# A ViT tower with a routed expert layer: a row table in blocks of 112, a reordered last tile, earlier first weights

## What is computed

```python
h = tok(x)                                   # layernorm, projection, layernorm, class row, positions
h = h + attn(layernorm(h))                   # q k^T / 256, diagonal masked, softmax, v
xf = layernorm(h)
topv, topi = top_k(softmax(xf @ router_w + router_b), 2); topv /= topv.sum()
pv, pp = top_k(where(flat_i == expert, flat_v, -1), 444)      # for each of the 8 experts
tok = pp // 2
out_e = (gelu(xf[tok] @ w1 + b1) @ w2 + b2) * pv              # 256 -> 1024 -> 256
out = layernorm(zeros.at[tok].add(out_e)) * ln_g + ln_b
h = h + out
```

## Time and profile before

| | before |
|---|---|
| median of 3 runs | 412.13 us (410.66 to 412.42) |
| the profiled execution | 415.01 us, of which the span from first to last instruction is 413.1 us |
| busy | PE 348.5 us (84%), DVE 315.5 (76%), ACT 255.3 (62%), POOL 224.1 (54%) |
| mean granted TensorE clock | 0.913 |
| DMA | 57.29 MB, mean 139 GB/s |
| chain that ended last, by engine | PE 60%, DVE 14%, issue 10%, POOL 8%, ACT 4% |
| its largest lines | L994 18%, L977 17%, L837 6%, L1290 2%, L805 2%, L812 2%, L939 2% |

### The profile page before, as it was taken

The page is one execution under the profiler, slowest core; times in us unless marked ns, Lnnn a source line. Parts: engine busy times, 40 slices in busy tenths (PEclk is TensorE's granted clock), DMA queues, the critical chain, the costliest instruction groups (busy, mean ns, idle before and its releaser), DMA issues.

```text
span 413.1 us, 7904 instructions
## 1 busy us (share of the span) xinstructions
PE 348.5 (84%) x2128; PEld 307.3 (74%) x2128; DVE 315.5 (76%) x874; ACT 255.3 (62%) x552; POOL 224.1 (54%) x377
## 2 busy tenths in 40 slices
PE   2799999999999998731019899999999999999960
PEld 0499988878878886431009899999999999999950
DVE  6763788787878877679879755778888888787954
ACT  3263778767777785454710478677777776868620
POOL 3243676756667665340005443158686877755675
PEclk9896999999999999865555999999999999999995
DMA  6650114454444479768702496546758585852231
GB/s 185 173 115 12 35 55 110 136 154 129 138 141 129 122 123 108 186 198 268 20 0 68 119 274 190 161 151 179 216 173 236 166 235 169 250 169 64 60 84 45
DMA packets 49278, 57.29 MB, mean 139 GB/s; under 512 B 12248, under 2 KB 38229, under 8 KB 49244
## 3 DMA queue, kind: packets, MB, share of 16 engines
q1 hardware_dynamic: 42602, 43.11, 39.4%
q0 software_dynamic: 5568, 13.00, 11.8%
q10 hardware_dynamic: 1074, 0.79, 0.8%
HBM read 36.74 MB, written 21.36 MB: 141 GB/s over the span
## 4 chain that ended last, share of the span: by engine, by line
PE 60%; DVE 14%; issue 10%; POOL 8%; ACT 4%; DMA 1%; ACTq 1%; DVEq 1%; POOLq 0%
PE pall L994 18%; PE pz L977 17%; PE pall L837 6%; DVE wproj L1290 2%; PE pall L805 2%; POOL held L1630 2%; PE pall L812 2%; PE pall L939 2%; PE pall L1005 1%; ACT stage L576 1%; PE pz L785 1%; POOL nrm L1609 1%; PE pall L963 1%; DMA bproj<-in_b_proj 1%; PE pall L777 1%
## 5 line engine op out<-in xcount | busy, mean ns | idle before, releaser
L994 PE MATMUL pall<-halves 128*128 128x444 f32 x384 | 88.6, 365 | 1.9 <-DVE halves L1398 1.9
L977 PE MATMUL pz<-halves 128*128 128x444 f32 x384 | 87.1, 362 | 0.1
L994 PEld LDWEIGHTS pall<-halves 128*128 128x128 f32 x384 | 70.8, 188 | 7.0 <-issue 1.5
L977 PEld LDWEIGHTS pz<-halves 128*128 128x128 f32 x384 | 71.9, 188 | 5.1 <-DVE halves L1409 0.2
L1649 POOL DMA_INDIRECT held<-x_rows,gidx x32 | 36.9, 1152 | 58.8 <-DVE gidx L1339 38.2
L738 ACT ACTIVATE wproj<-pz,b1t 128x444 f32<-128x444 f32 x64 | 40.5, 633 | 44.0 <-PE pz L977 43.4
L1398 DVE TENSOR_TENSOR halves<-wproj,halves 128x444 fp32r<-128x444 f32 x64 | 39.7, 621 | 27.1 <-ACT halves L750 18.7
L837 PE MATMUL pall<-halves 128*112 128x256 f32 x396 | 56.1, 298 | 3.1 <-DVE halves L1089 3.1
L837 PEld LDWEIGHTS pall<-halves 128*112 128x112 f32 x396 | 51.2, 186 | 7.2 <-DVE halves L1089 3.5
L1673 POOL DMA_INDIRECT out<-rows,didx x28 | 37.0, 1323 | 22.1 <-DVE rows L1446 15.5
L750 ACT CAST halves<-wproj 128x444 fp32r<-128x444 f32 x64 | 36.1, 564 | 2.0
(11 more groups left out here) (283 smaller groups left out, 744.5 us busy)
## 6 DMA issues: line engine op xcount, KB each, us to landing
stage<-in_w SPq DMA_DIRECT2D x32, 512.0 KB
stage<-in_x SPq DMA_DIRECT2D x64, 108.0 KB
x_rows<-x SPq DMA_DIRECT2D x22, 224.0 KB, 2.9
x_rows<-held SPq DMA_DIRECT2D x22, 224.0 KB, 4.1
sums<-rows SPq DMA_DIRECT2D x7, 448.0 KB
out<-held SPq DMA_DIRECT2D x21, 111.0 KB
x_rows<-zero SPq DMA_DIRECT2D x1, 1474.9 KB
wproj<-in_w_proj ACTq DMA_DIRECT2D x1, 768.0 KB
```

The costliest lines, as they stand in the source:

```text
L977: m = nc.tensor.matmul(bank(k % 2)[:, 0:CAP], w[:, c, k * 128:(k + 1) * 128], xs[:, e % 2, c, 0:CAP], start=(n == 0), stop=(n == 3 * EC - 1))
L994: m = nc.tensor.matmul(pall[:, 2 * (e % 2) + o, 0:CAP], w[:, k, o * 128:(o + 1) * 128], hs[:, k % 2, 0:CAP], start=(k == 0 and n == 0), st ...
```

## The change

1. **Row table.** The table has blocks of 112 rows (`P`) in place of 128, so no row of it is unused. The store of zeros at L499 goes, and `s_fill` is awaited at 32. The code of a row changes with it (`codef`, `code0`), and `read_lists` works out the block by a multiplication and a rounding in place of a mask and a shift: three more DVE instructions, each waiting for the one in front.
2. **First weights.** SP issues the four transfers of expert 0's weights at the top of step 22, ahead of that step's stores. ACT's four high halves move from the search's rounds behind its two tables.
3. **Gates.** The first gate stores move to step 24, ahead of its stores, the others to step 26; each keeps its wait on `r_V`.
4. **ACT's order.** At step 21 the scaled z of tile 21 comes ahead of x1 of tile 20. At step 22 the exponentials of tile 20 and the copy of x1T of tile 21 come directly behind x1 of tile 21, ahead of logits, x2 row and `h_rw`.
5. **POOL's order.** At step 22 POOL makes the factors of h of tile 21 alone, without waiting for tile 18's statistics, and `h_nb` before `h_dev`; tile 18's factors follow. The bias adds (L1624): tile 19's moves from step 25 to step 23 (beside tile 18's); those of tiles 20 and 21 come at step 26 behind a new wait on `r_V` = 2. Before, tiles 19 and 20 were at step 25 and tile 21 at step 26, with no such wait.

```diff
-        x2_rows = nc.dram_tensor("x2_rows", [(Q + 2) * 128, XW], fp32, kind="Internal").ap()
+        x2_rows = nc.dram_tensor("x2_rows", [(Q + 2) * P, XW], fp32, kind="Internal").ap()
@@ SP
             def step(i, slot):
                 par = slot % 2
+                if isinstance(i, int) and i == TILES:
+                    sp.wait_ge(x_n, TILES)
+                    sp.wait_ge(xT_ps, TILES)
+                    sp.wait_ge(z_ps, TILES)
+                    for h in range(2):
+                        load_w1(0, h)
+                        load_w2(0, h)
+                if isinstance(i, int) and i == TILES + 2:
+                    sp.wait_ge(r_V, 1)
+                    store_gates(0, EARLY)
+                if isinstance(i, int) and i == TILES + 4:
+                    sp.wait_ge(r_V, 2)
+                    store_gates(EARLY, TILES)
...
-                    sp.dma_start(x2_blocks[P:128, :, :],
-                                 rep(zero[0:128 - P, 0:XW].rearrange("p (a f) -> p a f", a=1), 1, Q + 2)).then_inc(s_fill, 16)
...
-            for h in range(2):
-                load_w1(0, h)
-                load_w2(0, h)
-            for a, b, n in ((0, EARLY, 1), (EARLY, TILES, 2)):
-                sp.wait_ge(r_V, n)
-                store_gates(a, b)
@@ ACT
+                last = isinstance(i, int) and i == TILES
+                if live(i - 1) and not (isinstance(i, int) and i == TILES - 1):
+                    residual_row(i - 1)
+                if last:
+                    exponentials(i - 2)
+                    turned(i - 1)
                 t = i
                 if live(t):
                     plain(act, (z_2, t + 1), (n_rs, i + 1))
                     nc.scalar.activation(tile_of(H, t), z2[:, :], ACT.Copy, scale=norm(par, 1, 0)).then_inc(z_sc, 1)
+                if isinstance(i, int) and i == TILES - 1:
+                    residual_row(i - 1)
...
             for r in range(NR - 1):
                 signs_of(r)
-                if r >= 3:
-                    (w2_high if r % 2 == 0 else w1_high)(0, (r - 3) // 2)
...
+            for pr in range(2):
+                w1_high(0, pr)
+                w2_high(0, pr)
@@ DVE, read_lists
-                V_.tensor_scalar(drow[:, 0, :], gidx[:, :], 127, None, ALU.bitwise_and)
-                link(V_.tensor_scalar(drow[:, 1, :], gidx[:, :], 8, None, ALU.logical_shift_right))
+                block_f = drow[:, 1, :].bitcast(fp32)
+                link(V_.tensor_scalar(block_f, gidx[:, :], -(P - 1) / 2.0, 1.0 / P, ALU.add, ALU.mult))
+                link(V_.tensor_scalar(block_f, block_f, BIG, None, ALU.add))
+                link(V_.tensor_scalar(drow[:, 0, :], block_f, -BIG, None, ALU.add))
+                V_.tensor_scalar(drow[:, 1, :], drow[:, 0, :], 1, None, ALU.logical_shift_right)
+                link(V_.scalar_tensor_tensor(drow[:, 0, :], drow[:, 0, :], -float(P), gidx[:, :], ALU.mult, ALU.add))
@@ POOL
+                if isinstance(i, int) and i == TILES:
+                    on = [2]
+                    pool.wait_ge(x1_ok, i - 2)
+                    pool.wait_ge(h_rw, i - 2)
+                    pool.wait_ge(h_mv, i)
+                    link(G.tensor_scalar(nrm[:, par, 0, 1:2], nmv[:, 1:2, 1], EPS, None, ALU.add))
+                    link(G.tensor_tensor(nrm[:, par, 1, 1:2], nrm[:, par, 0, 1:2], neghalf[:, :], ALU.pow))
+                    G.tensor_scalar(norm(par, 2, 1), nmv[:, 1, 0:1], norm(par, 1, 1), -1.0, ALU.mult, ALU.mult).then_inc(h_nb, 1)
+                    G.tensor_tensor(dev[:, par:par + 1], norm(par, 0, 1), norm(par, 1, 1), ALU.mult).then_inc(h_dev, 1)
...
-                for t in range(i - 6, i - 4) if isinstance(i, int) and i == TILES + 3 else (i - 5,):
-                    if live(t) and not (isinstance(i, int) and i == TILES + 2):
+                if isinstance(i, int) and i == TILES + 4:
+                    pool.wait_ge(r_V, 2)
+                for t in {TILES + 1: (i - 5, i - 4), TILES + 2: (), TILES + 3: (), TILES + 4: (i - 6, i - 5)}.get(i, (i - 5,)) \
+                        if isinstance(i, int) else (i - 5,):
+                    if live(t):
```

More of the change, by code:

```diff
@@ L475, in _, with load_w1, load_w2 @@
                 load_x(t, t)
+            HALF_H, HALF_K = HID // 2, HC // 2
+            def load_w1(e, h):
+                cols = slice(h * HALF_H, (h + 1) * HALF_H)
+                sp.dma_start(w1r[:, :, cols], w1[e].rearrange("(c p) h -> p c h", p=128)[:, :, cols])\
+                    .then_inc(w1_in[h], 16)
+            def load_w2(e, h):
+                ks = slice(h * HALF_K, (h + 1) * HALF_K)
+                sp.dma_start(w2r[:, ks, :], w2[e].rearrange("(k p) o -> p k o", p=128)[:, ks, :])\
+                    .then_inc(w2_in[h], 16)
             def step(i, slot):
                 par = slot % 2
+                if isinstance(i, int) and i == TILES:
[11 more added lines that the diff above has]
+                    store_gates(EARLY, TILES)
                 t = i + 4
@@ L555, in _ @@
             sp.wait_ge(s_out, 16 * (E - 1))
-            sp.wait_ge(s_fill, 48)
+            sp.wait_ge(s_fill, 32)
             sp.wait_ge(g_col, 64)
@@ L637, in step, with turned, exponentials @@
                                          scale=norm(par, 1, 1)).then_inc(x1_ok, 1)
+                def turned(t):
+                    need(act, x1T_ps, t + 1)
+                    need(act, s_ps, t - 1)
+                    nc.scalar.copy(x1T[:, odd, :], bank(6)[:, 0:EC * P]).then_inc(x1T_sb, 1)
+                def exponentials(t):
+                    need(act, s_nmx, t + 1)
+                    need(act, pT_ps, t)
+                    need(act, g_h, t - 1)
+                    nc.scalar.activation(prob[:, :], masked[:, :], ACT.Exp, bias=nmax[:, 0:1], scale=1.0 / ED,
+                                         accum_out=psumr[:, par:par + 1]).then_inc(p_ok, 1)
+                last = isinstance(i, int) and i == TILES
[4 more added lines that the diff above has]
+                    turned(i - 1)
                 t = i
@@ L660, in step @@
                     norm_row(t, slot, par)
-                t = i - 2
-                if live(t):
-                    need(act, s_nmx, t + 1)
-                    need(act, pT_ps, t)
-                    need(act, g_h, t - 1)
-                    nc.scalar.activation(prob[:, :], masked[:, :], ACT.Exp, bias=nmax[:, 0:1], scale=1.0 / ED,
-                                         accum_out=psumr[:, par:par + 1]).then_inc(p_ok, 1)
+                if live(i - 2) and not last:
+                    exponentials(i - 2)
                 t = i - 2
@@ L672, in step @@
                         .then_inc(h_rw, 1)
-                t = i - 1
-                if live(t):
-                    need(act, x1T_ps, t + 1)
-                    need(act, s_ps, t - 1)
-                    nc.scalar.copy(x1T[:, odd, :], bank(6)[:, 0:EC * P]).then_inc(x1T_sb, 1)
+                if live(i - 1) and not last:
+                    turned(i - 1)
             pipeline(act, step, 6, 18)
@@ L1273, in _ @@
                              ALU.mult, ALU.add)
-            V_.scalar_tensor_tensor(code0[:, :].bitcast(u16), oh12[:, 1, 0, :], 128.0, codef[:, 0:TILES], ALU.mult, ALU.add)
+            V_.scalar_tensor_tensor(code0[:, :].bitcast(u16), oh12[:, 1, 0, :], float(P), codef[:, 0:TILES], ALU.mult, ALU.add)
             dve.wait_ge(r_ka, 1)
@@ L1640, in _ @@
                 pool.wait_ge(x2_out[k], 16 * ((TILES - k + 3) // 4))
-            pool.wait_ge(s_fill, 48)
+            pool.wait_ge(s_fill, 32)
             pool.wait_ge(g_col, 64)
```

19 lines of the change are left out of this document (3 added, 16 removed).

## The result

The changed kernel took 410.63 us (median of 22 runs) where the kernel before, on the same chip, took 412.63 (22 runs): a ratio of 0.9933, interval 0.9909 to 0.9957. One of the 22 was disturbed (705.23 us) and counts for nothing. The difference of the medians is 2.0 us, the ratio gives 2.8. The forecast of 410.1 and its range hold. The profiled execution took 411.50 us, its span 409.7, against 415.01 and 413.1.

What follows compares the result with a forecast made beforehand. Bound before 235 us by a chain of waits, PE with the last tile's products, then DVE's routing. Terms 1.4 + 1.1 - 0 - 0.7 = 1.8, or 2.3; 2.0 taken from 412.13 gives 410.1 us, range 409.4 to 410.8 (8 in 10: 408.4 to 412.2).

Steps and rivals of the forecast that it cites:

- rival 1: Last tile's products: TensorE holds the high clock through L829, so 3.0 to 3.5 us faster, 409.0 us; chance 0.17.
- better case: Whole sum: 2.3 us faster if the clock falls at the same time and the adds miss the gates.
- x1 and L805: Last tile, step 22: x1, exponentials and x1T copy come earlier, so PE's L805 starts 1.4 us earlier.
- Products behind it: Last tile's products after L805: 1.4 to 2.3 us won, about 2.0 taken at the end of L829.
- Gates: DVE's gates of 16 tiles now meet two POOL adds: 0.6 us given back, bounds 0 and 1.2.
- Adds out of the routing: L1132, L1135 and L1136 in the last tiles' routing no longer run beside POOL's adds: 1.1 us won.
- Adds behind `r_V` = 2: Adds beside `keysa`: nothing to 0.7 us lost, 0 taken, since POOL needs 0.2 us to wake and `keysa` starts first.
- rival 3: At `keysa`: POOL's add gets in first and `keysa` waits for all of it, 0.7 us less gain, 410.8; chance 0.07.
- `read_lists`: Three more linked DVE instructions ahead of the first `project`: 0.66 us lost, bounds 0.5 and 0.9.
- rival 4: Gap before L994 grows to 1.8 us, TensorE's clock falls, first expert's products cost 3.7 us more, 413.8; chance 0.05.
- The fill, the weights, the gates: nothing: SP's zero fill, first weights and gate stores: no gain, as POOL's 38 us idle before the first gather covers them.

Runs made afterwards that it cites:

- G: Changed kernel with SP's old order: first weights and all gate stores behind the pipeline, no fill, blocks of 112; 409.93 us, 0.9918 to the kernel before.
- H: Changed kernel with ACT's and POOL's old order at steps 21 and 22, POOL's adds as changed; 412.67 us, 0.9993 to the kernel before.
- D: Kernel before with three redundant linked shifts added in `read_lists`, to lengthen the gap before the first `project`; 413.77 us, 1.0011 to the kernel before.
- I: Changed kernel with POOL's bias adds back at their old steps, no wait on `r_V`; 410.96 us, 0.9959 to the kernel before.
- J: Changed kernel with all four bias adds, tiles 18 to 21, behind `r_V` = 2; 410.57 us, 0.9934 to the kernel before.
- C: Changed kernel with nine idle matmuls on PE between `hidden(0, 1)` and the first `project`; 410.30 us, 0.9923 to the kernel before.
- A: The changed kernel again, unedited, for a second profile; 409.33 us, 0.9918 to the kernel before.
- K: Changed kernel with 29 idle matmuls in place of 24 ahead of the first gathered rows; 411.16 us, 0.9936 to the kernel before.
- B: Changed kernel with the second half of `read_lists` (nine operations) moved into the first expert; 408.73 us, 0.9898 to the kernel before.
- L: Changed kernel with lists as in B, adds as in J, tile 21's exponentials before an x2 row, third `hidden` before `project`; 407.83 us, 0.9853 to the kernel before.
- E: Changed kernel with the old row table: blocks of 128, zero fill, mask and shift; 415.14 us, 1.0037 to the kernel before.
- F: Changed kernel with the old row table and zero fill, and SP's old order too; 415.05 us, 1.0030 to the kernel before.

## Why the prediction was right, and where its steps were off

The time is right, and the bottleneck was read rightly: only the stretch between the last tile and the first expert counts, and from the first `by_slot` to the end nothing moved (155.64 and 155.70). That the forecast lies so close is in part luck. One term was too small by 1.2, a price in the first expert (1.6, in some executions) was left to a rival, and the two cancel. In G, which differs from the changed kernel in SP's order alone and whose clock held there, the stages give 3.2 us, which is the sum of rival 1 (3.0 to 3.5), not the forecast's 2.0. The written sum has a slip too: its 1.4 is the 2.0 of the products less the 0.6 of the gates, and its better case, 2.3 with the gates missed, adds to 2.3 + 1.1 - 0.7 = 2.7 and not 2.3.

**x1 and L805: right.** 1.4 forecast, 1.56 measured, by the steps named. H takes them away and L805 is back at 11.47.

**Products behind it: mis-sized, 2.0 taken, 3.2 measured** at the end of L829. The failed part is what I gave for the lower level: 0.9 us at most, on L812 alone. L821 and L829 stood at it as well. From L805's start to L829's end it was 4.58 us, now 2.93; an earlier tile had taken 2.94 at the high level (159.30 to 162.24). I also let the clock fall at 171 us or with the work. It did neither. Behind the last projection it fell at 12.3 us before and at 16.5 us as changed, and that is no chance of one execution: in the eleven profiles with the new orders it fell at 15.0 to 18.1 us, in the three with the old ones (before, D, H) at 11.0 to 12.4. PE's gaps ahead of the last tile had shrunk, as rival 1 says; that the gaps are what held the clock is argued, not tested by itself. Rival 1's argument against itself, that DVE and the adds cap the gain near 1.7, was wrong: L1132 came 2.52 earlier. DVE is the limit now, and carries 0.33 us that no term had: L1150 takes 0.62 for a usual 0.29 beside POOL's add at 166.28 (0.62 in I and J too, 0.29 in H with POOL's old order).

**Gates: right.** 0.6 forecast, 0.55 measured, and J removes it. That it would then be of no use was not foreseen, because the next wait, PE's for ACT, stood only 0.4 us behind.

**Adds out of the routing: right.** 1.1 against 1.14, and I brings it back.

**Adds behind `r_V` = 2: right, nothing, but not for the reason given.** POOL's wake-up was not 0.2 us but 0.09, from the end of L1177 at 181.84. The row of each engine in the changed kernel:

```profile
181.93 1.90 POOL L1655 TENSOR_TENSOR held<-held,lnb 112x256 f32<-112x256 f32 x2 [6.02 <-DVE V L1177]
```

```profile
181.95 0.62 DVE L1291 TENSOR_SCALAR keysa<-scratch 128x896 int32<-128x896 int32 x1
```

POOL is recorded 0.02 us ahead of `keysa`, and still `keysa` takes its 0.62 us. The loser is POOL: two adds in 1.90 us (the first 1.21, the second 0.73), where three took 2.10 before. From `keysa` to the index it is 32.59 us against 32.60. So rival 3 is excluded. The Trainium skill (SBUF — State Buffer, section "Who interferes with whom") says that such a DVE instruction and a GpSimd one exclude each other and that the first keeps the port. That they exclude each other agrees with POOL's longer time; who came first can't be told from records 0.02 us apart.

**`read_lists`: right.** 0.66 forecast, 0.68 from the first `hidden` to the first `project` (3.79 to 4.47), and 0.81 for a similar three steps in D.

**The clock in the gap: rival 4's mechanism came, its size and its condition did not.** It was priced at 3.7 us from a stretch of 7.4; it lasted 3.4 us and cost 1.6 (C). The condition, "only if a gap of 1.8 us is enough", does not hold by itself: five profiles with a gap of 1.80 to 1.93 us held 1.00 behind it. All eight with such a gap, the clock's changes read in narrow windows:

| | clock back at 1.00, behind the gather's issue | wait at the gather | at 1.00 before the gap | gap | fell |
|---|---|---|---|---|---|
| A | 1.9 us | 0.98 | 11.2 us | 1.81 | yes |
| J | 2.6 | 0.77 | 10.7 | 1.82 | yes |
| changed | 2.6 | 0.66 | 10.55 | 1.80 | yes |
| I | 2.9 | 0.52 | 10.25 | 1.81 | no |
| K | 4.0 | none | 10.0 | 1.80 | no |
| G | 3.9 | 0.10 | 9.3 | 1.81 | no |
| H | 5.0 | none | 8.4 | 1.81 | no |
| D | 4.8 | none | 8.4 | 1.93 | no |

While writing the experiments I read this as two idle stretches that must come together, 0.66 us or more at the gather and 1.8 ahead of `project`. The table allows that, but the first is no free choice: the earlier the clock rises again in the idle matmuls, the sooner these run out and the longer PE waits for the rows. So the wait at the gather, the early rise and the longer time at the high level go together here, and no run parts them. B, C and K can't do it: in them the clock came back 4.0 to 4.2 us behind the gather's issue, where G keeps it with nothing filled. Only L, back at 1.00 already 2.1 us behind the issue, with 1.06 us at the gather and no gap, speaks for the gap being needed. In E and F, with 2.6 us at the gather, the clock fell right there. What decides between fall and no fall stays open. On how often it comes the times say something: the three profiled executions that fell lie 0.7 to 2.6 us above the median of their own kernel's runs, those of B, C, E to I, K and L between 0.6 below and 0.2 above. So most runs seem to go without it.

**The fill: the step that failed.** "The fill, the weights, the gates: nothing" holds only against the kernel before as it stood. I read 38.19 us of idle POOL as cover and wrote that it would have to shrink by more than 12 us before a late store showed. But that idle time says when POOL was last busy, not when the last store landed. In the kernel before, the last gate store was issued at 199.85 and was the slowest of the four. Its own landing (the line's view, from 200 to 201 us):

```profile
DMA to landing us min/median/max: 15.6/15.6/15.6
```

It landed at 215.5, 5.0 us ahead of the gather at 220.50 and not 12, and the changed kernel gathers at 215.00, start-up included. With the fill and the earlier routing, E and F have their last store landed at 218.1, and the first `hidden` comes 5.0 us late: more than the whole gain. So the cost that the prediction put at nothing is this wait, as soon as the orders bring the gather forward. The backlog was also read too small: behind the fill the longest issue took 4.69 us (156.92), not 3.87. Removing the fill without the new orders was not tried; by the 5.0 us of slack it should gain nothing at the gather. H comes nearest, without the fill and with ACT's and POOL's old orders: 0.9993, with the 1.1 of the adds and the 0.7 of the lists in it.

**What is left open.** 1.8 of the 3.4 us between the spans lie before the last projection, where the change touches nothing that I can name. In the start-up TensorE is at the low level in other stretches (18 to 22 us: 0.67 before, 0.80 changed; 30 to 34: 0.61 and 0.91), and all twelve profiles of the other kernels reach the last projection at 156.0 to 157.0, the two of before (with D) at 158.2 and 158.5. But those two lie high among the runs of their kernels, 2.4 and 1.8 us above the median, so a part of the 1.8 may be the choice of the execution. By the stages alone the changed kernel gains 1.6 us with the fall and 3.2 without; the ratio gives 2.8, between 1.8 and 3.8. My 2.0 is inside, and which share of it is start-up isn't settled.

## What to carry to other kernels

A cost that hides under a wait now can come out when a second edit shortens the wait: before calling a slow queue covered, compute when its last transfer lands and subtract that from when it is asked for, with the other edits' shift already applied. Idle time of the waiting engine is not slack. Here it was 38 us of idle time and 5.0 us of slack. Where a chain of single operations closes a stage, moving one tile's operations ahead of older tiles' work was worth more than its own length (1.56 at the first product, 3.2 at the last), since TensorE kept its clock through what follows. For a gap that the change opens elsewhere, moving work out of its way (B, L) shortened it by 0.9 us and more; idle matmuls (C, K) gave nothing in the medians. And a single profile in which the clock fell or held says little on why: see when it last rose, before crediting the edit.

## What was not expected of the hardware

- TensorE's fall from 1.00 to 0.50 in the first expert did not follow from one gap of 1.8 to 1.9 us (five profiles without), and stood in the three profiles in which the clock had come back soonest and PE had waited 0.66 us or more for the gather some 6 us earlier.
- The gate stores, which write one number to each row, hold their issuing queue. The two at 172.63 held SP for 8.12 us and two more at 184.79 for 8.47, where an x2 or h store is issued in 0.3 to 0.5 in quiet stretches. That it is the short pieces, and not the traffic around them, was not tested:

```profile
172.63 8.12 SPq L450 DMA_DIRECT2D x_rows<-gate  x2
...
184.79 8.47 SPq L450 DMA_DIRECT2D x_rows<-gate  x2
```

- The fill of 1475 KB was issued in 0.7 us, but the four issues behind its follower took 3.9 to 4.7 us each (4.69 at 154.88 in E).
- A small DVE operation that meets a POOL add can lose the whole rest of it. POOL's two adds of the changed kernel stand at 170.37 to 171.09 and 171.18 to 171.92. L1167 starts in the first and ends at 171.12 (0.32 for a usual 0.17), L1169 starts in the second and ends at 172.07 (0.70 for 0.29). L1168, of the same kind, starts between them and takes its usual 0.18.
